# Second feed-forward of a macaron block: from gathers through an inverse table to rows scattered to their slots during the attention

## What is computed

```python
logits = layernorm(x) @ wg                    # 8 experts
topv, topi = top_k(softmax(logits), 2); topv /= topv.sum(-1)
flat = one_hot(topi.T, 8).reshape(2 * 4096, 8)        # first choices, then second ones
pos = ((cumsum(flat, 0) - 1) * flat).sum(-1)          # place within the expert
valid = pos < 1024                                    # capacity
disp[topi, pos] = layernorm(x) * valid                # 8 x 1024 slots
h = relu(disp @ w1 + b1); y = h @ w2 + b2             # 128 -> 512 -> 128 per expert
x = x + 0.5 * sum(gate * y[topi, pos])
```

## Time and profile before

| | us |
|---|---|
| median of 3 runs | 563.53 (558.3 to 564.83) |
| the profiled execution: its own time | 564.55 |
| the profiled execution: span of its instructions | 562.8 |

### The profile page before, as it was taken

One profiled execution on the slowest core, in us unless ns is written; L12 is line 12 of the kernel. 1 busy time (PEld: TensorE's weight loads), 2 busy tenths in 40 slices (PEclk: granted clock), 3 DMA queues, 4 the chain that ended last, 5 costly groups with the idle time before them and its releaser, 6 DMA issues. The chain is left out here.

```text
span 562.8 us, 5936 instructions
## 1 busy us (share of the span) xinstructions
PE 360.4 (64%) x1703; PEld 287.2 (51%) x1703; DVE 354.5 (63%) x1065; ACT 245.3 (44%) x454; POOL 267.4 (48%) x296
## 2 busy tenths in 40 slices
PE   7824589999992046877888412957677576548700
PEld 7702468888871025765766211746466465446500
DVE  6797479778873426767768793556356174246773
ACT  3683256776660024543453881245143153144400
POOL 7003777566402764655500004717747667747740
PEclk9999999999997566887879755678778879869955
DMA  8900115444433111111100041201112111101299
GB/s 242 361 16 10 50 46 165 141 133 136 146 131 103 51 52 29 42 44 38 37 1 2 1 152 30 52 14 48 49 31 53 47 38 53 47 24 47 64 323 286
DMA packets 40176, 46.93 MB, mean 83 GB/s; under 512 B 6262, under 2 KB 26768, under 8 KB 40144
## 3 DMA queue, kind: packets, MB, share of 16 engines
q1 hardware_dynamic: 27264, 27.30, 14.6%
q0 software_dynamic: 8512, 17.15, 11.6%
q10 hardware_dynamic: 4368, 2.10, 1.3%
HBM read 25.52 MB, written 21.00 MB: 83 GB/s over the span
## 5 line engine op out<-in xcount | busy, mean ns | idle before, releaser
L895 ACT ACTIVATE hf<-psum,bcol 128x512 f32<-128x512 f32 x128 | 87.6, 691 | 110.9 <-PE psum L836 41.3
L932 DVE TENSOR_TENSOR hl<-hf,hh 128x512 fp32r<-128x512 f32 x128 | 88.1, 696 | 22.9 <-ACT hh L897 13.3
L782 POOL DMA_INDIRECT xg<-xw_dram,gidx x64 | 62.4, 975 | 84.2 <-POOLq L1543 65.0
L808 POOL DMA_INDIRECT xg<-xn_dram,gidx x64 | 65.8, 1028 | 72.6 <-POOLq L1397 39.8
L791 POOL DMA_INDIRECT yt_dram<-y_sb,target x64 | 67.9, 1061 | 49.7 <-DVE y_sb L948 31.2
L1036 POOL DMA_INDIRECT yg<-y_dram,slot x64 | 61.0, 953 | 38.1 <-DVE x_sb L1233 19.9
L834 PE MATMUL psum<-xh,wres 128*128 128x512 f32 x128 | 59.3, 464 | 19.6 <-DVE xl L921 14.3
L925 DVE CAST hh<-hf 128x512 fp32r<-128x512 f32 x96 | 42.3, 440 | 34.0 <-ACT hf L895 33.6
L847 PE MATMUL psum<-hh,wres 128*128 128x512 f32 x128 | 55.6, 434 | 0.0
L835 PE MATMUL psum<-xl,wres 128*128 128x512 f32 x128 | 55.0, 430 | 0.0
L836 PE MATMUL psum<-xh,wres 128*128 128x512 f32 x128 | 55.0, 430 | 0.0
(11 more groups left out here) (202 smaller groups left out, 730.7 us busy)
## 6 DMA issues: line engine op xcount, KB each, us to landing
yt_dram<-zeros SPq DMA_DIRECT2D x24, 256.0 KB
ring<-yt_dram SPq DMA_DIRECT2D x24, 256.0 KB
wexp_raw<-in_L_ffn_w SPq DMA_DIRECT2D x16, 256.0 KB, 6.0
y_dram<-y_sb SPq DMA_DIRECT2D x16, 256.0 KB
xw_dram<-xns SPq DMA_DIRECT2D x8, 260.0 KB, 2.9
x_sb<-in_L_attn_x SPq DMA_DIRECT2D x8, 256.0 KB, 3.8
xn_dram<-xns SPq DMA_DIRECT2D x8, 256.0 KB, 5.7
out<-x_sb ACTq DMA_DIRECT2D x8, 256.0 KB, 5.6
```

The costliest lines, as they stand in the source:

```text
L782: gp.indirect_dma_start(out=self.xg[:, s % XG, t], out_offset=None, in_=xw_dram, in_offset=bass.IndirectOffsetOnAxis(ap=gidx[:, j:j + 1], ...
L808: gp.indirect_dma_start(out=self.xg[:, s % 4, t], out_offset=None, in_=xn_dram, in_offset=bass.IndirectOffsetOnAxis(ap=gidx[:, j:j + 1], a ...
L895: one = nc.scalar.activation(self.hf[:, c], bank[1 + c][:], ACT.Relu, bias=bcol[:, at:at + 1])
L932: dve.tensor_tensor(self.hl[:, s % 2, c], self.hf[:, c], self.hh[:, s % 2, c].bitcast(F32), ALU.subtract).then_inc(hl_ready[c], 1)
```

## The change

1. **Ranking in one half each.** `PARTS` is now (0, 4, 8) for both feed-forwards. The scale of the rows of groups 0 to 3 is made beside step 6 of the attention's loop and their ranking beside step 7, no longer in the drain.
2. **Places instead of an inverse table.** `place_steps` gives for each choice of a token its slot (or a row beyond the slots where the expert is full). The first choices of groups 0 to 3 depend on no later token, so PE counts them in the drain (`early_counts`, 128 columns). The rest (16 tiles of first choices and 32 of second ones) follows behind the last logits (`late_counts`). `chosen_token`, `lo`, `hi_tok`, the 64 products, `gidx` and `xw_dram` are gone for the second feed-forward, and so is the block that held them.
3. **Dispatch.** POOL scatters the normalized rows with two more columns (gate and target row in `yt_dram`) to `xs_dram`, 64 indirect DMAs of 128 rows: first choices of groups 0 to 3, first choices of groups 4 to 7, then all second choices. The two columns lie in `xns` itself, so DVE rewrites them (`second_marks`) once the first scatter of that half has landed.
4. **Plain loads.** SP loads each superblock in one DMA of 260 KB (`sync_rows`, first wait: all scatters landed). POOL keeps only the 64 scatters of outputs. DVE turns the target column to integers, one copy of 4 columns per superblock, in place of three small gate operations.
5. **Clearing.** `xs_dram` is filled with blank rows in the first feed-forward: one more SP store of 260 KB per superblock. POOL makes the blank tile at the start (memset of 2080 columns).

The diff, cut to its core:

```diff
-EARLY = (NG // 2, NG - 2)
-PARTS = ((0, NG // 2, NG), (0, NG // 2, NG - 2, NG))
+EARLY = NG // 2
+PARTS = (0, NG // 2, NG)
...
+            def early_counts(self, pe):
+                n = GT * EARLY
+                pe.wait_ge(first_chosen, 1)
+                pe.wait_ge(qT_ready, NG)
+                by_expert = self.choice[:, 0:n].rearrange("p j e -> p e j")
+                nc.tensor.matmul(bank[1][:, 0:E * n]..., tri[:], by_expert, start=True, stop=True)
+                nc.tensor.matmul(bank[1][:, 256:256 + E * n]..., ones_bf[:], by_expert, ...).then_inc(counts_done, 1)
...
+            def dispatch(self, gp):
+                for part in range(2):
+                    gp.wait_ge(rows_placed, part + 1)
+                    gp.wait_ge(first_marked, 2 * part + 2)
+                    for g in range(PARTS[part], PARTS[part + 1]):
+                        gp.wait_ge(norm_act, NG + g + 1)
+                        for t in range(GT * g, GT * g + GT):
+                            gp.indirect_dma_start(out=xs_dram, out_offset=bass.IndirectOffsetOnAxis(ap=self.place[:, t:t + 1], axis=0),
+                                                  in_=self.xns[:, g, t % GT], in_offset=None).then_inc(firsts_in[part], 16)
+                for part in range(2):
+                    gp.wait_ge(second_marked, 2 * part + 2)
+                    for t in range(GT * PARTS[part], GT * PARTS[part + 1]):
+                        gp.indirect_dma_start(out=xs_dram, ...place[:, NT + t:NT + t + 1]..., in_=self.xns[:, t // GT, t % GT], in_offset=None).then_inc(seconds_in, 16)
...
+            def sync_rows(self, sp):
+                sp.wait_ge(firsts_in[1], 16 * GT * (NG - EARLY))
+                sp.wait_ge(seconds_in, 16 * NT)
+                for s in range(NSB):
+                    if s >= XG:
+                        sp.wait_ge(y_ready, NSB + s - XG + 1)
+                        sp.wait_ge(targets_known, s - XG + 1)
+                    sp.dma_start(self.xg[:, s % XG], token_rows(xs_dram, s * SEQ)).then_inc(slot_rows_in[s % XG], 16)
...
-                for s in range(AHEAD):
-                    gather(s)
                 for s in range(NSB):
-                    scatter(s)
-                    if s + AHEAD < NSB:
-                        gather(s + AHEAD)
+                    gp.wait_ge(targets_known, s + 1)
+                    gp.wait_ge(y_ready, NSB + s + 1)
...
-                        last = dve.tensor_scalar(self.y_sb[:, s % YG, t], bank[6][:, t * P:(t + 1) * P], self.gs[:, s % YG, t:t + 1], None, ALU.mult)
+                        last = dve.tensor_scalar(self.y_sb[:, s % YG, t], bank[6][:, t * P:(t + 1) * P], self.xg[:, s % XG, t, C:C + 1], None, ALU.mult)
...
-                finish(ranks)
+                finish(route.place_steps(dve, ch, 0))
                 k_sum(NG - 1)
-                advance(scalars, 8)
+                finish(route.first_marks(dve, ch, 0))
                 kv_mask(NG - 1)
```

More of the change, by code:

```diff
@@ L544, in top2_steps @@
                 f = self.f
-                first, end = PARTS[f][part], PARTS[f][part + 1]
-                last_part = part == len(PARTS[f]) - 2
+                first, end = PARTS[part], PARTS[part + 1]
+                last_part = end == NG
                 ts = slice(GT * first, GT * end)
@@ new lines, in second_marks @@
+            def second_marks(self, dve, part):
+                ts = self.tiles_of(part)
+                by_row = lambda a: a.rearrange("p (g t) -> p g t", t=GT)
+                second = slice(NT + ts.start, NT + ts.stop)
+                dve.wait_ge(firsts_in[part], 16 * GT * EARLY)
+                dve.scalar_tensor_tensor(self.marks(part, 1), by_row(self.choice[:, second, E - 1]), 1.0 * N, by_row(token_row[:, 1, ts]), ALU.mult, ALU.add).then_inc(second_marked, 1)
+                dve.scalar_tensor_tensor(self.marks(part, 0), by_row(gap[:, ts]), 0.5, by_row(e2[:, ts]), ALU.mult, ALU.mult).then_inc(second_marked, 1)
@@ L1345, in vector @@
                         k_sum(s - 1)
-                    finish(scale)
+                    for _ in scale:
+                        advance(others, pace)
                     if s >= 1:
                         kv_mask(s - 1)
+                    finish(others)
                     if s + 1 < NG:
@@ L1498, in _ @@
                     else:
-                        experts.gather_and_scatter(gp)
+                        experts.scatter(gp)
                 @block.tensor
@@ L1529, in _ @@
                 gather.gpsimd(gp)
+                route1.dispatch(gp)
             @block.tensor
```

301 lines of the change are left out of this document (173 added, 128 removed).

## The result

The changed kernel takes 555.96 us (median of 5 runs, 555.31 to 564.32) against 563.53; the ratio is 0.988, 95% interval 0.984 to 0.991. I had forecast 541 (0.960). Measured is 7.6 us less than before, by my own measure (2%) no change. The ratios leave disturbed runs out and can differ a little from those of the medians.

What follows compares the result with a forecast made beforehand. POOL's indirect DMAs were taken to bound the second expert stage. First transpose +46.2, stage -68.6 and end -0.7 gave -23.1 us: span 539.7, forecast 541 us (4% less), range 532 to 563.

Steps and rivals of the forecast that it cites:

- Second half ready: Attention's drain: statistics, ranking, counts and positions of the second half; POOL goes on with its scatters at 330.4.
- Landing: Between the last scatter of the dispatch and SP's first load: rows land in 1.35 us.
- the 0.8 us more: First load: by the Trainium skill's 2.15 us for a 66 KB POOL DMA instead of 1.35, added once.
- Front and shift: First experts' blank stores cost 0.7 us (0 to 1.5); steps moved into the attention's loop delay the drain 3.0 (0 to 6.6).
- Stage and end: Second expert stage takes 115.7 us like the first (bounds 111 and 121), then 28.5 us to the end.
- the first rival: Second expert stage: ACT's unexplained waits stay, 42 us on top, own time 583; chance 0.11 in full, 0.07 in half.
- ACT's waits in the stage: Second expert stage: 33.3 us "remote" at the hidden layer, some 12 at others, read as following a starved PE and fallen clock.
- Slow scatters beside DVE: Dispatch: first 16 scatters beside busy DVE take 3 us each, time 572, no change; chance 0.05.
- Loads didn't lag: Second expert stage: rival that PE finds no superblock because loads lag, so POOL's relief is worth nothing; chance 0.02.
- Within 2%: Whole kernel: outcome of no change beyond 2%, chance 0.13, against 0.75 faster (below 552) and 0.12 slower.
- halves of other rivals: Whole kernel: half of ACT's waits staying gives 562 (chance 0.07); slow scatters (0.05) fall mostly within 2%.

Runs made afterwards that it cites:

- a_third: The changed kernel again, unaltered, on chip R beside the kernel before: 556.97 us, ratio 0.994.
- a_fourth: The changed kernel again, unaltered, on chip Q beside the kernel before: 522.53 us, ratio 1.023.
- steps_back: Changed kernel with the 20 scale and 12 ranking steps of the first half back behind the attention's loop on DVE; chip Q: 529.04 us, ratio 1.035.
- later_block: Changed kernel with the dispatch after the first 16 scatters moved into the second expert stage's block; chip Q: 520.90 us, ratio 1.021.
- block_and_clear: Changed kernel with all but the first 16 scatters in the experts' block and blank stores behind the attention's first gathers; chip R: 551.83 us, ratio 0.986.
- before_more: The kernel before the change again, unaltered, on chip Q: 511.11 us, ratio 1.002.
- scatter_twice: Changed kernel with each output row of the second expert stage scattered a second time, to an unread tensor; chip P: 643.68 us, one run.
- later_block_p: Changed kernel with all but the first 16 scatters in the experts' block, and three 0.5 us memsets behind every four first-half scatters; chip Q: 527.12 us, ratio 1.036.

## Why the prediction was wrong, step by step

| us | forecast | first profile | a_third | a_fourth (Q) |
|---|---|---|---|---|
| POOL's first scatter | 307.1 | 315.8 | 308.0 | 285.6 |
| from it to POOL's second half | 23.3 | 35.1 | 35.2 | 21.9 |
| 48 scatters | 61.1 | 61.0 | 60.8 | 60.8 |
| last scatter to first load | 1.35 | 7.9 | 7.9 | 7.9 |
| load to first transpose | 2.65 | 3.35 | 2.7 | 3.3 |
| experts | 115.7 | 111.3 | 110.7 | 111.2 |
| end | 28.5 | 27.8 | 27.8 | 28.0 |

- **"Second half ready" failed.** I had summed instructions (DVE steps, two products) with no wait on a signal, and put POOL's first 16 scatters beside them as free. They aren't: unbroken, they delay the signals between PE, ACT and DVE, and the part is 11.8 and 11.9 us longer in the two profiles. What stands there instead is POOL's row of 20.2 us, 2.5 us more until the last late copy, and the 12.5 us from it over logits, ranking and positions to POOL's second half: 35.2. In a_third (clock 0.53 there) some 5 of the 11.9 us are not lateness but the clock, for which my sum had no term: at 0.50 with every signal on time the part takes 28.2 us (steps_back) for my 23.3, the late signals add the other 7. That the sum is right within 1.4 us in a_fourth (21.9) is luck in this respect: its clock was 0.74.
- **"Landing" failed.** I read 1.35 us from a wait inside one block and put it on a load behind a block's end. The landing is 1.4 us as read (later_block, block_and_clear); POOL's DRAIN adds 6.5. From its start a scatter takes 2.3 us to land, 1.3 behind its end, so the 0.8 us more that the prediction speaks of were not owed. The trace of before has the DRAIN: at the attention's end the last gather is issued by 278.0 and POOL's DRAIN ends at 283.3, at the first experts' end 149.6 and 154.9, both hidden by other engines.

```profile
L1522 POOLq DRAIN  x1: 11044/11044/11044, 272.3 to 272.3; - x1
```

- **Front and shift.** The stores cost 1.4 us for my 0.7. The loop with the moved steps is 5.6 us longer on Q (99.6 against 94.0), within my 0 to 6.6 but not my 3.0, and 0.7 on R (119.4 against 118.7). But on the late chips the changed loop takes from 119.4 to 124.0 us by the execution, so that POOL's first scatter in a_third is only 0.9 us off is in part chance. In the first profile the start stood 4.2 us later besides: 1.5 of it the stores, 2.4 a longer first expert stage.
- **Stage and end.** 111 for 115.7, at the lower bound, 27.8 for 28.5. The pattern that I took, the first stage of before, had late signals in it: ACT has 5.0 us of "remote" waits between 73 and 79 us, beside POOL's first row of 20 gathers and just ahead of the window from 81 to 163 that I held against the first rival. Without them the first stage takes 111.8 us (before_more), the same as the new one, and DVE is no bound. On a_third the misses sum to 0.9 + 11.9 - 0.3 + 6.6 - 5.0 - 0.7 = 13.4, which is 553.1 - 539.7.
- **Rivals.** ACT's waits in the stage did not stay; but my reason ("what follows a starved PE and a fallen clock") was wrong. In the changed stage PE starts just as starved, at 1.2 GHz (its first transposes take 1.12 us as before), and they are gone; scatter_twice brings them back. Had I read them as what a POOL without pauses does, the new place for them, the drain, was plain to see. Slow scatters beside DVE: 0.97 to 1.01 us, so that rival fell. The Trainium skill (SBUF — State Buffer, two separate sides) gives some 3100 ns for a DMA of POOL beside a `tensor_copy` of DVE; nothing of the kind is seen beside the steps of this drain, and whether any of them is of the sort that the page means, no run shows. Loads didn't lag.
- **The likelier outcome was left out of the cases.** "Within 2%" had 0.13, from halves of other rivals; no case had the dispatch delaying the work beside it.

## What to carry to other kernels

Idle time that the profile calls "remote" or "issue" wants its own explanation before work is moved, and before a stage that has some of it serves as the pattern for another: hold each waiter's start against the end of the work that it waits for, and ask what else runs in those stretches and not in the quiet ones. Long rows of indirect DMAs from POOL are not free beside a chain of short steps between PE, ACT and DVE; measure the gain on more than one chip. And where a block ends behind indirect DMAs, look for POOL's DRAIN, or put them into the block of their consumer, which waits for the rows alone.

## What the runs showed of the hardware that was not expected

- On the first chip, P and R, PE's signals reached ACT and DVE up to 8.4 us late in rows of 16 and more indirect DMAs of POOL that stand 0.30 us apart, and DVE's signals to DVE itself up to 2.6 us late (a_third, 209.31). In groups of four with 1.3 us between (changed expert stage) no wait was "remote", nor with 1.8 us of memset between groups of four in the drain. On chip Q none was in eight whole profiles. The kernel before differs by 54 us between Q and R, in the stretches with such rows. What in the chip does this was not found: the profile records the semaphore updates late, and what holds them up isn't seen.
- POOL's DRAIN ends 5.3 to 7.6 us after the issue of the last indirect DMA has ended (149.6 to 154.9, 278.0 to 283.3, 411.9 to 419.4; 8.5 in later_block_p, 311.1 to 319.6), though the rows land after 1.3 us (413.2 in the first profile).
- On chip Q the same drain of 72 products takes 23.6 or 29.8 us by where the clock falls from 2.4 to 1.2 GHz in it (granted 0.74 and 0.50 over it). With late signals it takes 36.7 to 37.0 at either.
